# A one-element exponential ahead of the attention pairs, and one of six output tiles added by GpSimd from a copy that ScalarE makes

## What is computed

```python
scores = jnp.einsum('hnd,hmd->hnm', q2, k2) * scale + mask[None]
attn = jax.nn.softmax(scores, axis=-1)
...
base = jnp.einsum('btd,od->bto', x, base_W) + base_b
h = jax.nn.relu(jnp.einsum('btd,bdr->btr', x, Wd) + bd[:, None, :])
a = jnp.einsum('btr,brd->btd', h, Wu) + bu[:, None, :]
y = jnp.einsum('btd,bod->bto', a, Wc) + bc[:, None, :]
return base + y
```

## Time and profile before

| | |
|---|---|
| median of 3 runs | 472.8 us (472.56 to 473.14) |
| the profiled execution's own time | 472.28 us |
| its span (first to last recorded instruction) | 470.5 us |
| PE busy | 462.7 us (98%) |
| DVE, ACT, POOL busy | 341.7, 258.7, 153.4 us |
| granted clock of TensorE, mean | 0.998 |
| chain that ended last, by engine | PE 91%, DMA 2%, DVE 2%, ACT 2% |

### The profile page before, as it was taken

How to read it: one execution, slowest core, us unless ns; L and a number is a source line. 1 busy time by engine, 2 the same in 40 slices (tenths; PEclk the granted TensorE clock), 3 DMA queues, 4 the chain that set the end, 5 groups by cost and what they waited for, 6 DMA issues and landing times.

```text
span 470.5 us, 7320 instructions
## 1 busy us (share of the span) xinstructions
PE 462.7 (98%) x2521; PEld 429.9 (91%) x2521; DVE 341.7 (73%) x787; ACT 258.7 (55%) x423; POOL 153.4 (33%) x178
## 2 busy tenths in 40 slices
PE   7999999999999999999999999999999999999996
PEld 5999999999999888999999999999998888888885
DVE  6979876776636347688888888897875993586394
ACT  3724533333314244878979698897965362153270
POOL 4246667767777761001010202202044000050200
PEclk9999999999999999999999999999999999999999
DMA  8877776566544465477676747767669854210553
GB/s 247 324 235 213 233 213 168 180 181 184 155 131 159 129 206 197 156 236 262 198 226 205 240 154 228 246 211 232 195 210 364 276 214 135 89 45 1 169 236 134
DMA packets 39097, 91.92 MB, mean 195 GB/s; under 512 B 7458, under 2 KB 20354, under 8 KB 38932
## 3 DMA queue, kind: packets, MB, share of 16 engines
q1 hardware_dynamic: 33540, 83.02, 55.9%
q0 software_dynamic: 4864, 7.45, 4.7%
q10 hardware_dynamic: 656, 0.98, 0.6%
HBM read 77.96 MB, written 13.47 MB: 194 GB/s over the span
## 4 chain that ended last, share of the span: by engine, by line
PE 91%; DMA 2%; DVE 2%; ACT 2%; SPq 1%; issue 0%; DVEq 0%; ACTq 0%
PE PS L1327 34%; PE PS L1337 28%; PE PS L1332 17%; PE PS L1465 4%; PE PS L1453 2%; PE PS L1589 2%; PE PS L1395 2%; DMA U<-x 1%; PE PS L1315 1%; ACT U L684 1%; PE PS L1593 1%; DVE U L1303 1%; PE PS L1573 1%; DMA turn<-U 1%; DMA U<-turn 1%; ACT w_hi L561 0%
## 5 line engine op out<-in xcount | busy, mean ns | idle before, releaser
L936 DVE TENSOR_TENSOR w_lo<-raw,w_hi 128x1024 fp32r<-128x1024 f32 x86 | 104.3, 1225 | 45.8 <-ACT w_hi L561 45.7
L561 ACT ACTIVATE w_hi<-raw 128x1024 fp32r<-128x1024 f32 x87 | 91.0, 1054 | 72.8 <-PE PS L1337 46.0
L477 POOL DMA_INDIRECT table<-evalue,where x96 | 102.5, 1068 | 42.5 <-issue 26.0
L1332 PE MATMUL PS<-xT_hi,w_lo 128*128 128x384 f32 x320 | 61.9, 334 | 0.0
L1327 PE MATMUL PS<-xT_lo,w_hi 128*128 128x384 f32 x320 | 61.9, 334 | 0.0
L1327 PE MATMUL PS<-xT_hi,w_hi 128*128 128x384 f32 x320 | 61.9, 334 | 0.0
L1332 PEld LDWEIGHTS PS<-xT_hi,w_lo 128*128 128x128 f32 x320 | 56.0, 188 | 0.0
L1327 PEld LDWEIGHTS PS<-xT_lo,w_hi 128*128 128x128 f32 x320 | 56.0, 188 | 0.0
L1327 PEld LDWEIGHTS PS<-xT_hi,w_hi 128*128 128x128 f32 x320 | 56.0, 188 | 0.0
L1337 PE MATMUL PS<-w_hi,T_hi 128*128 128x512 f32 x144 | 40.1, 391 | 0.0
L1337 PE MATMUL PS<-w_hi,T_lo 128*128 128x512 f32 x144 | 39.9, 389 | 0.0
(11 more groups left out here) (247 smaller groups left out, 805.4 us busy)
## 6 DMA issues: line engine op xcount, KB each, us to landing
raw<-weights SPq DMA_DIRECT2D x84, 512.0 KB, 4.6
turn<-U SPq DMA_DIRECT2D x16, 576.0 KB, 3.8
U<-turn SPq DMA_DIRECT2D x64, 144.0 KB, 2.9
U<-key_dram SPq DMA_DIRECT2D x32, 192.0 KB, 4.2
mask<-weights SPq DMA_DIRECT2D x9, 512.0 KB, 5.1
table<-Q POOLq DMA_DIRECT2D x4, 576.0 KB
V<-conv SPq DMA_DIRECT2D x4, 512.0 KB, 5.1
U<-table POOLq DMA_DIRECT2D x3, 576.0 KB, 6.6
```

The source lines that it names most:

```text
L477: pool.indirect_dma_start(tables[g], bass.IndirectOffsetOnAxis(ap=where[:, k:k + 1], axis=0), evalue[:, k:k + 1], None, bounds_check=N * N ...
L561: act.activation(w_hi[slot][:], raw[slot][:], ACT.Copy).then_inc(hi_ready[slot], 1)
L936: dve.tensor_tensor(w_lo[slot][:], raw[slot][:], w_hi[slot][:].bitcast(F32), ALU.subtract).then_inc(lo_ready[slot], 1)
L1332: last = pe.matmul(o, wl, src[0][:, k, :], start=False, stop=(k == KB - 1))
```

## The change

There are two edits. First, ACT gets one more activation, an exponential of one column, written ahead of `v2_out(1)`; the result is not used. Second, the output tile (half 0, rows 0) is no longer added by DVE: ACT copies it from PSUM to a free part of `Q2` (`y_copy`) once `y_done` is 1, and GpSimd adds the copy to the rows of `x` and counts `y_pooled`. DVE adds the other five tiles. SP stores the tiles in the order (0, 1), (0, 2), (0, 0), (1, 0), (1, 1), and the half of (1, 2); ACT's last store waits for the fifth add of DVE.

```diff
+        y_copy = Q2[:].rearrange("p k n -> p (k n)")[:, 2 * D:2 * D + HALF]
...
-            for half in range(2):
-                c = slice(half * HALF, (half + 1) * HALF)
-                for t in range(NT):
-                    sp.wait_ge(y_ready, half * NT + t + 1)
-                    mine = P if half * NT + t < 2 * NT - 1 else SP_ROWS
-                    sp.dma_start(out[t * P:t * P + mine, c], x_rows[0:mine, t, c]).then_inc(stored, 16)
+            for t in (1, 2):
+                sp.wait_ge(y_ready, t)
+                store(t, slice(0, HALF))
+            sp.wait_ge(y_pooled, 1)
+            store(0, slice(0, HALF))
+            for t in range(2):
+                sp.wait_ge(y_ready, t + 3)
+                store(t, slice(HALF, D))
+            sp.wait_ge(y_ready, 5)
+            sp.dma_start(out[2 * P:2 * P + SP_ROWS, HALF:D], x_rows[0:SP_ROWS, 2, HALF:D]).then_inc(stored, 16)
...
             split_lo(*E_USES[7])
+
+            pool.wait_ge(y_copied, 1)
+            pool.tensor_tensor(x_rows[:, 0, 0:HALF], y_copy, x_rows[:, 0, 0:HALF], ALU.add).then_inc(y_pooled, 1)
...
+            act.activation(tiny[:, 24:25], tiny[:, 0:1], ACT.Exp)
             v2_out(1)
...
-            act.wait_ge(y_ready, 2 * NT)
+            act.wait_ge(y_done, 1)
+            act.activation(y_copy, PS[:, E_BANKS[0][0], :], ACT.Copy).then_inc(y_copied, 1)
+            act.wait_ge(y_ready, 5)
             act.dma_start(out[2 * P + SP_ROWS:3 * P, HALF:D], x_rows[SP_ROWS:P, NT - 1, HALF:D]).then_inc(stored, 16)
...
-            final_rows(0)
-            final_rows(1)
+            for half, t in ((0, 1), (0, 2), (1, 0), (1, 1), (1, 2)):
+                final_rows(half, t)
```

More of the change, by code:

```diff
@@ L337, in gps_layer @@
         y_done = sem("y_done")
+        y_copied = sem("y_copied")
+        y_pooled = sem("y_pooled")
         y_ready = sem("y_ready")
@@ L429, in _, with store @@
                 load_weights(s, use, conv[ds(expert * 8 + b, 1)].rearrange("a p n -> (a p) n"))
-            for half in range(2):
-                c = slice(half * HALF, (half + 1) * HALF)
-                for t in range(NT):
-                    sp.wait_ge(y_ready, half * NT + t + 1)
-                    mine = P if half * NT + t < 2 * NT - 1 else SP_ROWS
-                    sp.dma_start(out[t * P:t * P + mine, c], x_rows[0:mine, t, c]).then_inc(stored, 16)
-            sp.wait_ge(stored, 16 * (2 * NT + 1))
+            def store(t, c):
+                sp.dma_start(out[t * P:(t + 1) * P, c], x_rows[:, t, c]).then_inc(stored, 16)
+            for t in (1, 2):
[8 more added lines that the diff above has]
+            sp.dma_start(out[2 * P:2 * P + SP_ROWS, HALF:D], x_rows[0:SP_ROWS, 2, HALF:D]).then_inc(stored, 16)
+            sp.wait_ge(stored, 16 * 7)
         @block.gpsimd
@@ L1297, in _, with final_rows @@
             split_p(1)
-            def final_rows(half):
+            def final_rows(half, t):
                 c = slice(half * HALF, (half + 1) * HALF)
[L1301 to L1304, removed]
-            final_rows(0)
-            final_rows(1)
+                dve.wait_ge(y_done, half * NT + t + 1)
+                dve.tensor_tensor(x_rows[:, t, c], PS[:, E_BANKS[half][t], :], x_rows[:, t, c],
+                                  ALU.add).then_inc(y_ready, 1)
+            for half, t in ((0, 1), (0, 2), (1, 0), (1, 1), (1, 2)):
+                final_rows(half, t)
         @block.tensor
```

## The result

The changed kernel takes 475.11 us (median of 6 runs, 474.88 to 476.05), the kernel before 472.97 (median of 6, 472.19 to 473.79): a ratio of 1.0052, 95% interval 1.0039 to 1.0065. The forecast was 472.5, 0.3 us faster, with a range up to 473.3. The profiled execution has a span of 473.6 us (475.43 us in all) where the one of before has 470.5 (472.28).

A forecast was written before the change was run, and what follows sets the result against it. PE was taken as the bound (busy 462.7 of 470.5 us), so only its stops or time after its last matmul pay. Terms -0.43 and +0.15 take 472.8 to 472.5 us, range 471.9 to 473.3.

The forecast's parts named there:

- part 2: Output tiles at the end: GpSimd's add, 1.34 us, is in time; stores start and land 0.15 us later, +0.15 us.
- the end follows from the first store: Tail: DMA engines limit the stores without a hole, so the last lands 0.15 us later, like the first.
- Rival C: Tail: GpSimd's add takes above 2.0 us and holds three stores behind it; 472.85, far end 474.05 us; chance 0.07.
- Part 1: Table load moves to ACT's idle stretch, first exponential 1.30 us earlier; PE's two stops in pair 1 go, -0.43 us.
- From there on PE never waits for anything that keeps its own time: Behind pair 1's stops PE has no such waits, so all of the 0.43 us gained is carried to the end.
- Rival A: Tail: the end follows the last add, not the bytes ahead, and moves by -0.12 us; 472.25 us; chance 0.22.
- Rival B: Earlier blocks' write meets weight slabs, takes its median or more; table gain falls to 0.26 or nothing; 472.7-472.95 us; chance 0.18.
- Rival D: Whole change does nothing, as the table load and the tail would both be hidden; 472.8 us; chance 0.05.

## Why the prediction was wrong

**The step that failed** is in part 2: "the end follows from the first store". I asked which engine is waited for by the stores, and took SP's wait for the stores to be the end of the program. GpSimd's close had no term in the sum at all. But the program also has to wait until GpSimd has drained, and that takes 8.5 us from where GpSimd reaches it. In the kernel before, GpSimd is done 30 us ahead, so the drain (to 448.37) was hidden, with 470.3 - 448.4 = 21.9 us to spare. The edit put a GpSimd instruction that waits for PE's first output tile behind this cover: 464.90 + 8.51 = 473.41, which is 3.1 us behind the point at which SP was through (470.3). Rival C was about GpSimd, but with the wrong price and place: it held GpSimd's add for the danger, to be decided at 2.0 us of duration. The add took 1.29 us (1.34 forecast) and was in time. The point from which GpSimd decides is another: its last step must end before 470.3 - 8.5 = 461.8 us, and PE's first output tile comes at 463.0. No add on GpSimd behind an output tile, however short, could have been free.

**The size.** Between the two profiles it is 3.14 us of span: +3.29 in the tail (7.34 less 4.05) and -0.15 that PE had earlier, from before pair 0. The medians differ by 2.14. The profiled execution of before was 0.7 us under its median of six, the one of the change 0.3 over; that is the difference (3.15 - 0.7 - 0.3 = 2.15). Stops such as that of pair 5, which come and go, are part of this scatter; the rest of it was not traced.

**Part 1**: the load in the idle stretch (177.64, forecast 177.8), the first exponential at 187.46 where it was 189.02 (1.56 us earlier, 1.42 of it relative to PE), the distance in pair 1 down to 1.77 us: right. Between the two profiles nothing of it reached the end, since a stop of 0.40 us came up in pair 5; that was chance and not the edit, as the writes of the blocks show above. "From there on PE never waits for anything that keeps its own time" was wrong all the same: I took pairs 2 to 7 to be free of stops because the one profile of before had none, and over the traces that kept PE's order pair 5 takes 20.69 to 21.16 us from scores to scores, pair 6 up to 21.54. On the average of executions the term is about -0.3 in place of -0.43, for two reasons: pair 1's stop is 0.36 by the medians, and not the 0.43 of that profile, and the rest is scatter. The load ends at 178.92 and the next activation starts at 178.93, so at its new place too no drain is seen behind it.

**Part 2 up to the stores**: +0.23 against +0.15, the mechanism right, and the kernel with DVE in GpSimd's place shows it a second time by its hole. Rival A (the tail follows the last add) falls: the last add ended 0.73 us behind the last matmul in place of 0.86, and the stores still ended later. The 389 GB/s of the forecast is one window; the mean of the windows from 465.4 to 468.6 is about 380 GB/s before and in the change, so a tile takes 0.69 us, more than the 0.60 of DVE's old pace, and the backlog is real. The Trainium skill, "DMA: Bandwidth & Descriptors", section "Anatomy of one DMA — SWDGE (gpsimd) path", gives its 2.0 us plus bytes at 436 GB/s for transfers that GpSimd issues; the forecast used it for stores of SP and ACT without saying so. For these the trace does not agree: by that fit a tile alone would take 2.6 us to land, as an estimate, and the quickest here took 2.0.

**Rival B** was half right. The earlier write (pair 0, first head) did take longer, 3.1 to 3.7 us in all eleven traces with the early load where it took 2.8 in the nine without. But it was to decide from 0.87 us of extra time on, and only one trace got there: 3.69 us, and there pair 1's distance is 2.07. In the profile of the change the write took 3.10. **Rival D** (no change) falls with the loss of 2.1 us.

## What to carry to other kernels

Before work is moved to an engine that is idle at the end, look at what that engine still has to do to close the program: ask the trace for the line of the end, and read each engine's DRAIN as a duration, not only as a mark. On GpSimd it was 8.5 us in this program, so here GpSimd's last instruction, a bare wait included, has to be over 8.5 us before the last store lands; in the last stage, finish GpSimd's stream early and give late work to an engine whose closing drain is short.

A stop that is gone in one profile, on an engine that feeds a chain with no slack, is worth what several executions say of it, not what one says. And a stop that has turned up in another place is the edit's doing only if it comes with the edit more often than without.

## What the runs showed of the hardware that I had not expected

- GpSimd's closing DRAIN takes 8.48 to 8.51 us in all 20 traces, behind an add, a memset or a wait alone. The closing DRAINs of the others are short behind their last work: ACT 0.4 to 0.6 us, SP 0.013; DVE's 0.7 to 1.0 and PE's 2.3 to 2.7 are nearly all its last add and its last matmuls. At the program's beginning GpSimd's drain took 0.19 us. What it does in the 8.5 us, and whether the 109 transfers that GpSimd had issued have to do with it, was not tried.
- One memset of a column on an idle engine, with no one waiting for it, made the tail of this program 1.4 us longer, and a wait alone 4.9 us (4.2 in the time of the one execution, against the median of before).
- The seven stores of the end are one stream for the DMA engines, at about 380 GB/s (353 to 404 in the windows of 0.4 us at a full share): a hole of 0.52 us between two of them moved the end by 0.57, and a last add that ended 0.13 us earlier moved nothing forward.
- The two writes of blocks ahead of pair 5's product, of the same size in every execution, took 8.05 to 9.10 us together, and PE stopped there in each of the ten traces above 8.6 us and in none of the ten below 8.5.
